# A decoder layer's setup: context chunks transposed one ahead, six buffers for the keys' parts, the first normalisation's steps moved forward, and the first shift rows not loaded

## What is computed

```python
y = x @ U                                            # 128 -> 32
x = layernorm(x + softmax(-|y_i - y_j|^2) @ x)       # self-attention by distance
q, k, v = x @ Wq + bq, ctx @ Wk + bk, ctx @ Wv + bv  # 16 heads of 8
x = layernorm(x + softmax(q k^T / sqrt(8)) @ v @ Wo + bo)
x = layernorm(x + ffn(x))                            # fake-quantised weights and activations
```

## Time and profile before

| | |
|---|---|
| time, median of 3 runs | 802.47 us (802.28 to 802.56) |
| profiled execution, own time | 802.64 us |
| its span, first to last instruction | 800.9 us |
| mean granted TensorE clock | 0.967 |
| busy: PE, ACT, DVE, POOL | 87%, 90%, 76%, 22% of the span |
| setup's second half | about 50 to 80.9 us |
| first scores, first exponential | 80.91 us, 82.06 us |

### The profile page before, as it was taken

The page is one execution under the profiler, slowest core; times in us unless marked ns, Lnnn a source line. Parts: engine busy times, 40 slices in busy tenths (PEclk is TensorE's granted clock), DMA queues, the critical chain, the costliest instruction groups (busy, mean ns, idle before and its releaser), DMA issues.

```text
span 800.9 us, 36509 instructions
## 1 busy us (share of the span) xinstructions
PE 696.5 (87%) x15090; PEld 313.6 (39%) x15090; DVE 606.4 (76%) x1712; ACT 723.6 (90%) x629; POOL 176.4 (22%) x318
## 2 busy tenths in 40 slices
PE   8996899999999899999998989998999999899841
PEld 4554244434443344334433443344434443444321
DVE  4568488858887788678867888588868886788666
ACT  3555799999999999999999999999999999999641
POOL 3436222212221222212211222122212221222100
PEclk8999699999999999999999999999999999999975
DMA  4354211111111111111111111111111111111000
GB/s 137 112 151 144 67 43 36 38 41 42 39 37 38 46 43 35 40 45 42 35 41 46 43 35 36 45 42 38 38 41 46 38 35 41 39 35 36 3 0 26
DMA packets 36991, 38.35 MB, mean 48 GB/s; under 512 B 8942, under 2 KB 35472, under 8 KB 36896
## 3 DMA queue, kind: packets, MB, share of 16 engines
q1 hardware_dynamic: 35788, 36.59, 15.9%
q10 hardware_dynamic: 1108, 0.46, 0.2%
HBM read 30.13 MB, written 6.42 MB: 46 GB/s over the span
## 4 chain that ended last, share of the span: by engine, by line
ACT 57%; issue 27%; PE 11%; DVE 3%; ACTq 1%; DMA 1%; POOL 0%; DVEq 0%; POOLq 0%
ACT probs L754 56%; PE ps L1296 2%; PE ps L1250 2%; PE ps L1258 1%; PE ps L1417 1%; PE ps L1287 1%; PE ps L1387 1%; ACTq L767 1%; DMA wq_sb<-in_L_xattn_Wq_dram 1%; PE ps L1241 0%; DVE probs L1185 0%; ACTq L752 0%; ACT ctx_t L667 0%; DVE stats L820 0%; PE ps L1493 0%
## 5 line engine op out<-in xcount | busy, mean ns | idle before, releaser
L754 ACT ACTIVATE probs<-ps 128x1536 f32<-128x1536 f32 (+1 forms) x536 | 669.5, 1393 | 7.6 <-PE ps L1387 7.6
L1417 PE MATMUL ps<-probs,v_op 64*9 64x512 f32 (+1 forms) x8256 | 524.4, 498 | 0.0
L1387 PE MATMUL ps<-q_op,k_op 59*32 59x512 bf16 x6432 | 335.9, 383 | 65.2 <-ACT probs L754 62.4
L1387 PEld LDWEIGHTS ps<-q_op,k_op 59*32 59x32 bf16 x6432 | 103.7, 90 | 350.9 <-issue 260.7
L1045 DVE TENSOR_SCALAR e_t<-ps 128x256 f32<-128x256 f32 x240 | 90.6, 419 | 145.4 <-PE ps L1387 145.4
L1417 PEld LDWEIGHTS ps<-probs,v_op 64*9 64x9 f32 x8256 | 172.6, 86 | 61.7 <-issue 5.7
L630 POOL TENSOR_SCALAR e_pow<-e_t 128x512 int32<-128x512 int16 x120 | 74.3, 620 | 357.8 <-DVE e_t L1045 357.8
L623 POOL COPY v_op<-v_all 128x108 f32<-128x108 f32 x136 | 64.3, 473 | 171.3 <-PE ps L1417 170.7
L1073 DVE SCALAR_TENSOR_TENSOR e_f<-e_f,e_pow 128x256 f32<-128x256 f32 x240 | 98.6, 449 | 0.0
L1062 DVE SCALAR_TENSOR_TENSOR e_u<-e_f 128x256 f32<-128x256 f32 x240 | 90.0, 415 | 0.2
L1067 DVE SCALAR_TENSOR_TENSOR e_f<-e_u,e_f 128x256 f32<-128x256 f32 x240 | 90.1, 416 | 0.0
(11 more groups left out here) (190 smaller groups left out, 243.1 us busy)
## 6 DMA issues: line engine op xcount, KB each, us to landing
k_op<-k_parts_dram SPq DMA_DIRECT2D x544, 36.0 KB
k_parts_dram<-k_parts SPq DMA_DIRECT2D x17, 288.0 KB, 2.9
k_op<-k_parts_dram SPq DMA_DIRECT2D x272, 12.0 KB
ctx_nat<-in_ctx_dram SPq DMA_DIRECT2D x16, 192.0 KB, 2.6
q_op<-q_parts_dram SPq DMA_DIRECT2D x32, 48.0 KB
q_parts_dram<-q_parts SPq DMA_DIRECT2D x2, 384.0 KB, 3.3
x_nat<-in_x_dram SPq DMA_DIRECT2D x1, 512.0 KB, 3.8
o_t<-att_rows SPq DMA_DIRECT2D x28, 16.0 KB
```

The costliest lines, as they stand in the source:

```text
L754: act.activation(probs[:, b % NP].rearrange("p u t -> p (u t)")[:, 0:columns], ps[:, bank:bank + BU, :].rearrange("p u t -> p (u t)")[:, 0 ...
L1387: return pe.matmul(ps[a:a + P // G, bank, :], k_op[W2 * r:W2 * r + KR, kslot, i, P * j + a:P * j + a + P // G], q_op[W2 * r:W2 * r + KR, q ...
L1417: last = pe.matmul(ps[32 * k:32 * k + DH + 1, ACC[h], a:b], v_op[W2 * h:W2 * h + W2, slot, j, (DH + 1) * k:(DH + 1) * (k + 1)], probs[W2 * ...
```

## The change

**Chunks turned one ahead.** On PE `turn(n+1)` now stands before `project_keys(n)`. `ctx_t` has three slots, so `turn_ctx(n)` waits for the values of chunk n-3.

**Six buffers.** `k_parts` has six slots (KP), and `first_part(n)` waits for the store and the maximum of chunk n-6.

**Normalisation's steps first.** DVE does both halves of `residual`, one `second_part`, all statistics and the moments together, then reciprocal, shift and `x1`, with no chunk's work between them. DVE normalises tiles 0 to 4 (X1_DVE = 5), ACT tiles 5 to 7. ACT switches to the Sqrt table before it waits for the attention's output, and back to Exp between its copy of `x_t` and the first query part. From chunk 9 on all value copies are ACT's (9, 11, 13 and 15 were DVE's). DVE's `absolute` calls come later, and so does `second_part(16)`, which now follows the product of the maxima. `sig` (sigmoid of the clips) moves to the end of ACT's setup.

**Shift rows.** The first `load_q` leaves the two DMAs of shift rows out, so it is six DMAs on a semaphore of its own (`q_first_loaded`). On SP it now follows `store_k(11)`, the store of the queries' half 0 and `store_k(12)`; before it followed `store_k(11)` to `store_k(13)` and that store.

**The end on PE.** The transpose of `kq_max` stands before `project_values(16)` and the `bv` matmul, which it followed.

The diff, its core:

```diff
+Q_FIRST = 16 * 3 * R2
...
+KP = 6
...
+X1_DVE = 5
...
-ctx_t = sb("ctx_t", [P, 2, CK])
+ctx_t = sb("ctx_t", [P, 3, CK])
...
-k_parts = sb("k_parts", [P, 4, 3, CK], BF16)
+k_parts = sb("k_parts", [P, KP, 3, CK], BF16)
...
-k_parts_written = [sem(f"k_parts_written{i}") for i in range(4)]
+k_parts_written = [sem(f"k_parts_written{i}") for i in range(KP)]
...
-q_loaded = [sem("q_loaded0"), sem("q_loaded1")]
+q_loaded, q_first_loaded = [sem("q_loaded0"), sem("q_loaded1")], sem("q_first_loaded")
...
+def by_dve(n):
+    return n < TQ and n % 2 == 1
 def wait_values_copied(engine, n):
-    if n % 2:
-        engine.wait_ge(v_ready_dve, n // 2 + 1)
+    if by_dve(n):
+        engine.wait_ge(v_ready_dve, sum(by_dve(i) for i in range(n + 1)))
     else:
-        engine.wait_ge(v_ready_act, n // 2 + 1)
+        engine.wait_ge(v_ready_act, sum(not by_dve(i) for i in range(n + 1)))
...
-def load_q(sp, slot, half, group_rows, group, signal, counter=None, count=None, only=None):
+def load_q(sp, slot, half, group_rows, group, signal, counter=None, count=None, only=None,
+           shifts=True):
...
+                continue
+            if a == 56 and not shifts:
...
-        sp.dma_start(k_parts_dram[n].rearrange("a p t -> p a t"), k_parts[:, n % 4]
-                     ).then_inc(k_parts_written[n % 4], 16)
+        sp.dma_start(k_parts_dram[n].rearrange("a p t -> p a t"), k_parts[:, n % KP]
+                     ).then_inc(k_parts_written[n % KP], 16)
...
-    for n in range(NC - 6, NC - 3):
-        store_k(n)
+    store_k(NC - 6)
     store_q(0)
-    sp.wait_ge(zero_shift_written, 16)
+    store_k(NC - 5)
     sp.wait_ge(q_parts_written[0], 16)
-    load_q(sp, 0, 0, slice(0, 32), 0, q_loaded[0])
-    for n in range(NC - 3, NC):
+    load_q(sp, 0, 0, slice(0, 32), 0, q_first_loaded, shifts=False)
+    for n in range(NC - 4, NC):
...
+    sp.wait_ge(zero_shift_written, 16)
...
-        for slot in range(4):
-            sp.wait_ge(k_parts_written[slot], 16 * len(range(slot, NC, 4)))
+        for slot in range(KP):
+            sp.wait_ge(k_parts_written[slot], 16 * len(range(slot, NC, KP)))
...
+        sp.wait_ge(q_first_loaded, Q_FIRST)
...
-        pool.tensor_copy(k_parts[:, n % 4, 1, :], kr[:, n % 4, :]).then_inc(k_mid_ready, 1)
+        pool.tensor_copy(k_parts[:, n % KP, 1, :], kr[:, n % 4, :]).then_inc(k_mid_ready, 1)
         pool.wait_ge(k_mid_ready, n + 1)
-        pool.tensor_tensor(k_parts[:, n % 4, 2, :], kr[:, n % 4, :], k_parts[:, n % 4, 1, :],
+        pool.tensor_tensor(k_parts[:, n % KP, 2, :], kr[:, n % 4, :], k_parts[:, n % KP, 1, :],
...
-    pool.wait_ge(x1_dve, 1)
+    pool.wait_ge(x1_dve, 2)
...
-        if n >= 2:
-            act.wait_ge(v_projected, n - 1)
-        act.activation(ctx_t[:, n % 2, :], ps[:, turn_bank(n), 0:CK], ACT.Copy
+        if n >= 3:
+            act.wait_ge(v_projected, n - 2)
+        act.activation(ctx_t[:, n % 3, :], ps[:, turn_bank(n), 0:CK], ACT.Copy
...
-        if n >= 4:
-            act.wait_ge(k_parts_written[n % 4], 16 * (n // 4))
-            act.wait_ge(k_abs_ready, n - 3)
-        act.activation(k_parts[:, n % 4, 0, :], ps[:, k_bank(n), 0:CK], ACT.Identity,
+        if n >= KP:
+            act.wait_ge(k_parts_written[n % KP], 16 * (n // KP))
+            act.wait_ge(k_abs_ready, n - KP + 1)
+        act.activation(k_parts[:, n % KP, 0, :], ps[:, k_bank(n), 0:CK], ACT.Identity,
...
-    act.wait_ge(ffn_w_loaded, FFN_LOADS)
-    act.activation(sig[:], clips[:], ACT.Exp, scale=-1.0).then_inc(sig_ready, 1)
+    act.preload_act_table(ACT.Sqrt)
...
+    turn_ctx(9)
...
-    turn_ctx(9)
-    act.preload_act_table(ACT.Sqrt)
+    turn_ctx(10)
     first_part(9)
-    turn_ctx(10)
+    copy_values(9)
+    turn_ctx(11)
     first_part(10)
+    turn_ctx(12)
     copy_values(10)
-    turn_ctx(11)
-    first_part(11)
-    turn_ctx(12)
...
-    first_part(12)
     act.wait_ge(shift_ready, 1)
-    for j in range(TQ // 2, TQ):
+    for j in range(X1_DVE, TQ):
...
-    copy_values(12)
+    first_part(11)
+    copy_values(11)
...
-    first_part(13)
+    act.preload_act_table(ACT.Exp)
...
-    act.preload_act_table(ACT.Exp)
+    first_part(12)
     turn_ctx(14)
+    first_query_part(1)
+    copy_values(12)
+    first_part(13)
+    turn_ctx(15)
+    copy_values(13)
     first_part(14)
-    copy_values(14)
-    first_query_part(1)
-    turn_ctx(15)
...
+    copy_values(14)
+    copy_values(15)
     copy_values(16)
+    act.wait_ge(ffn_w_loaded, FFN_LOADS)
+    act.activation(sig[:], clips[:], ACT.Exp, scale=-1.0).then_inc(sig_ready, 1)
...
-                                 scalar=bias_cols[:, 0:1], in1=k_parts[:, n % 4, 0, :],
+                                 scalar=bias_cols[:, 0:1], in1=k_parts[:, n % KP, 0, :],
...
-        dve.tensor_reduce(k_abs[:, n:n + 1], k_parts[:, n % 4, 0, :], AX.X, ALU.max,
+        dve.tensor_reduce(k_abs[:, n:n + 1], k_parts[:, n % KP, 0, :], AX.X, ALU.max,
...
-        dve.wait_ge(res_ready, half + 1)
-        return spread(dve, range(4 * half, 4 * half + 4))
     residual(0)
+    residual(1)
     second_part(9)
-    copy_values(9)
-    chain.step(residual(1))
+    dve.wait_ge(res_ready, 2)
+    chain.step(spread(dve, range(TQ)))
     moments(dve).then_inc(var_ready, 1)
-    second_part(10)
-    absolute(8)
-    second_part(11)
-    copy_values(11)
...
-    normalise(dve, x1, range(TQ // 2)).then_inc(x1_dve, 1)
-    second_part(12)
-    for n in range(9, 12):
-        absolute(n)
+    normalise(dve, x1, range(4)).then_inc(x1_dve, 1)
+    normalise(dve, x1, range(4, X1_DVE)).then_inc(x1_dve, 1)
+    second_part(10)
+    absolute(8)
...
-    absolute(12)
-    second_part(13)
+    second_part(11)
+    absolute(9)
...
-    copy_values(13)
+    second_part(12)
+    absolute(10)
+    second_query_part(1)
+    second_part(13)
+    absolute(11)
+    absolute(12)
+    absolute_query(0)
...
-    second_query_part(1)
-    absolute_query(0)
-    absolute(14)
...
-    second_part(16)
+    absolute(14)
...
-    copy_values(15)
+    second_part(16)
...
-        pe.matmul(ps[:, k_bank(n), 0:CK], wk_turned[:], ctx_t[:, n % 2, :],
+        pe.matmul(ps[:, k_bank(n), 0:CK], wk_turned[:], ctx_t[:, n % 3, :],
...
-                             ctx_t[:, n % 2, P * j:P * j + P], wv_sb[:], start=True, stop=True)
+                             ctx_t[:, n % 3, P * j:P * j + P], wv_sb[:], start=True, stop=True)
...
+    turn(9)
     project_keys(8)
-    project_values(8)
-    turn(9)
...
-    for n in range(9, 13):
+    project_values(8)
+    for n in range(9, 12):
+        turn(n + 1)
...
-        turn(n + 1)
-    for half, ready in ((0, x1_dve), (1, x1_act)):
-        pe.wait_ge(ready, 1)
+    turn(13)
+    for half in range(2):
+        pe.wait_ge(x1_dve, half + 1)
+        if half:
+            pe.wait_ge(x1_act, 1)
...
-    project_keys(13)
...
+    project_keys(12)
...
+    turn(14)
+    project_queries(1, x1_t_dve)
+    project_values(12)
+    project_keys(13)
+    turn(15)
     project_values(13)
-    turn(14)
     project_keys(14)
-    project_values(14)
-    project_queries(1, x1_t_dve)
-    turn(15)
...
+    project_values(14)
     project_values(15)
+    pe.wait_ge(kq_ready, 1)
+    pe.transpose(ps[0:1, 2, 0:P], kq_max[:, 2:3], ident[:]).then_inc(bound_made, 1)
...
-    pe.wait_ge(kq_ready, 1)
-    pe.transpose(ps[0:1, 2, 0:P], kq_max[:, 2:3], ident[:]).then_inc(bound_made, 1)
...
-        pe.wait_ge(q_loaded[ph % 2], Q_LOAD * (ph // 2 + 1))
+        if ph == 0:
+            pe.wait_ge(q_first_loaded, Q_FIRST)
+        else:
+            pe.wait_ge(q_loaded[ph % 2], Q_LOAD * ((ph + 1) // 2))
...
```

## The result

The changed kernel took 797.11 us (median of 6 runs, 795.57 to 798.93), the kernel before 802.38 us (6 runs, 800.3 to 802.56) beside it: ratio 0.9945, 95% interval 0.993 to 0.996. With all later runs the distance is smaller: 21 runs of the changed kernel have their median at 797.29, 73 of the kernel before at 800.78, 3.5 us apart. Four of the first six runs of the kernel before lay at 802.3 to 802.6 us, where only 12 of the 67 later ones do.

A forecast was written before the change was run, and what follows sets the result against it. ACT's exponentials were taken to bound the main stage, so only an earlier start helps: scores at 78.5 instead of 80.91, 2.4 us, taken off the median 802.47, gave 800.1 us; range 798.3 to 802.8.

The forecast's parts named there:

- The walk: Setup's new queues laid out with old row durations: root 59.0, `kq_ready` 75.25, first scores 78.5, 2.4 us earlier.
- five tiles of `x1`: Normalisation on DVE: tiles 0 to 4 at 0.41 us each, from 59.7 to 61.7.
- the query's middle part: DVE's queue before the product of maxima: priced at 0.74 us, between query parts of 0.79 and 0.61.
- the Exp load ending before query half 0 does: Sign before the first query part: ACT's Exp load ends at 64.1, just under PE's query half 0 at 64.2.
- as long as nothing else changes: Main stage's start: each microsecond the first exponential comes sooner is one off the total, if the stretch behind it stays unchanged.
- case A: Whole kernel: the 2.4 us come off the total, 800.1 us on the median of 802.47; chance 0.50.
- Case D: Setup's end: PE's clock does not fall, first scores take 0.6 us, ACT lacks its 2.1 us of gaps; 797.6, chance 0.08.
- B: PE's hole around `x1`: the clock falls to half rate for 6.8 us, gain only 0.6 us; 801.9, chance 0.24.
- C: Same hole before `x1`: clock falls and stays down, scores 3.4 us later than before; 805.9, chance 0.08.
- Turning ahead: PE's chunk loop: takes 0.33 us per chunk out, but after 59 us worth nothing by itself.
- Shift rows and the load's place: Queries' first load on SP: six loads issued by 74.0, landing by 77.5, before scores at 78.5.
- the table load of 1.28: ACT's table switches: 1.28 us each, without the skill page's added drain of about 1.38.

The follow-up runs named there:

- u_copies: Changed kernel with filler matmuls of zeros wherever PE stood idle, value copies of chunks 9, 11, 13 and 15 back on DVE: 794.51 us, against 794.24 without that edit.
- u_turn: Changed kernel with filler matmuls wherever PE stood idle, turn n+1 again behind keys and values of chunk n for chunks 8 to 11: 797.16 us, against 794.24.
- u_norm: Changed kernel with filler matmuls wherever PE stood idle, second_part 10, absolute 8 and first_part 11 put back between moments and root: 794.80 us, against 794.24.
- u_qload: Changed kernel with filler matmuls wherever PE stood idle, queries' first load as before (eight DMAs with shift rows, behind store_k 13): 798.55 us, against 794.24.

## Why the prediction missed

- **Size of the sum.** The walk's times held. Counted from the attention's end, the root was forecast 59.0 and came at the equivalent of 58.9 (57.60 plus the 1.3 us of the front), query half 0's part at 64.9 and 64.7, `kq_ready` at 75.25 and 74.6, scores at 78.5 and 78.0. So the gain was 0.5 us larger than the sum. Two terms were too large: five tiles of `x1` at 0.41 each, 2.05, took 1.36, and the query's middle part took 0.43 instead of 0.71. Both rows of before had POOL at work beside them, and I carried a duration over without its neighbour. Of the tiles' 0.7 us only some 0.2 reached the query part: PE had query half 0 done by 62.4, but the Exp load ended at 62.63, so the sign "the Exp load ending before query half 0 does" came out the other way, and DVE waited 1.15 us, not half a microsecond.
- **The failed step** is the first paragraph's "as long as nothing else changes", and case A's sum on 802.47. I took the clock's stretches of one profile as the kernel's own, and three runs that lay within 0.3 us of each other as its time. That profile's mean clock, 0.967, was the lowest that the kernel before shows, in 12 of 67 runs; on its median of 800.78 the same 2.4 us give 798.4, which is inside the range. The 5.3 us add up so: 2.4 forecast, 0.5 by which the sum was too small, 0.6 of clock at setup's end (3.5 less 2.9) and 1.8 by which the first six runs of each kernel happened to differ more than all of them do (5.3 less 3.5). The front's stretch is chance: the copy of o_t starts at 51.8 with 6.8 us at half rate, at 50.5 with 3.4, and at 48.4 to 49.4 with none.
- **Case D at 0.08** named the right place but too little chance, and only its extreme form: the clock still fell, yet later or for shorter. Its 797.6 is the profiled run's time, 797.57, by luck: the first scores did take 0.64, but ACT kept 1.84 of its 2.1 us of gaps, and the front gave 1.3. That the new order gives PE two matmul groups right before the branch, which the walk itself has, was not turned into a chance.
- **Cases B and C** did not come true in the profiles of the changed kernel: the clock stayed at 1.00 through the hole before `x1`. A fall in a pause of PE did happen in u_copies, at 68.9, for 3.4 us, and cost about 1 us. So the danger that B names was real, but not in the hole before `x1`: PE was busy 2.11 of 3.30 us there (58.00 to 61.30), where the walk had about 1.5.
- **Turning ahead, "by itself it is worth nothing there",** was wrong as a statement about the change. The walk had the root at 59.0 only because ACT's queue came to it in time, and it came in time because of the turns. I credited the gain to the order of the norm's steps. u_turn shows 2.9 us for the turns, u_norm 0.5 for the part of the steps that it puts back, u_qload 2.35 for the load. Turns and load are limits beside each other, of which each alone holds back most of the gain, and such prices don't add up. The gain's number came near in spite of this, since the walk laid out the whole order.
- **Shift rows and the load's place, priced at nothing:** right for what it binds after the change (last issue at 71.8, scores at 76.7), but it hides that the old place would bind.
- **Held:** the table load of 1.28 with the next ACT row right behind (61.35 to 62.65), so no drain; the time at the branch, 1.8 us from `bo_bc`'s end against 1.67, with a clearing matmul inside it; the six buffers at nothing; the main stage unchanged.

## To carry over

When two parts of a change each keep a chain just below another one, undoing either can cost nearly the whole gain, so ask of each edit what the others would hit without it, not what it gives alone. Before comparing single profiles, read the granted clock of each stretch: here runs of one kernel fall on steps of 0.8 to 1.4 us that no code explains, and the comparison that told most was the one where fillers took these steps away. A row's duration on DVE has to be read with what POOL did beside it.

## What the runs showed of the hardware

**DVE beside POOL.** The same kind of DVE operation, on 128x2 elements, took 0.15 us and, while POOL worked on a 128x1024 addition, 2.1. In the timeline of the kernel before:

```profile
79.15 0.15 DVE L1021 TENSOR_SCALAR sig<-sig 128x2 f32<-128x2 f32 x1
79.30 2.34 POOL L606 TENSOR_TENSOR x_bo<-x,bo_bc 128x1024 f32<-128x1024 f32 x1 [0.32 <-DVE bo_bc L1019]
79.34 0.17 DVE L1022 RECIPROCAL sig<-sig 128x2 f32<-128x2 f32 x1
79.54 2.13 DVE L1023 TENSOR_SCALAR sig<-sig 128x2 f32<-128x2 f32 x1
```

POOL's and the second TENSOR_SCALAR both end at about 81.65. The reciprocal, 0.17 us beside POOL's, was not held. The five `x1` tiles took 1.36 us with POOL idle and 1.98 in u_norm, where a POOL operation of 0.91 us began just before them. The Trainium skill, "SBUF — State Buffer", section "🔬 SBUF: two separate sides", describes a port pair that DVE and GpSimd share as an exclusive lock; the trace agrees (2.13 us, ending with POOL's), and it is the likely reason why the two terms were mis-sized; that the wait is for this port pair no run here shows.

**The clock's chance.** With PE's front filled, the changed kernel's runs lay within 0.24 us (four) and 1.1 us (five), and eleven of the kernel before within 1.3; unfilled, 21 and 67 runs lay within 3.7 and 4.0. What was not settled: how many stretches at half rate a given order will have.
